# A decoder layer in one kernel: the first group's split and load orders, the weighting of c, q2c as columns, and where its products stand

## The reference, cut to what matters

```python
x = x + attn(layernorm(x))                       # attn: layernorm, q,k,v, softmax over channels, projection, + its input
# xattn(c = layernorm(x), q = ctx):
cq = jnp.einsum('bcd,bqd,d->bcq', c, q, w_cq) + b_cq
s = (c @ w_c + b_c)[:, :, None] + (q @ w_q + b_q)[:, None, :] + cq
a = jax.nn.softmax(s, axis=2)
c2q_att = jnp.einsum('bcq,bqd->bcd', a, q)
b_att = jax.nn.softmax(jnp.max(s, axis=2), axis=1)
q2c_att = jnp.einsum('bc,bcd->bd', b_att, c)[:, None, :]
z = jnp.concatenate([c, c2q_att, c * c2q_att, c * q2c_att], axis=-1) @ W_l.T + b_l
x = x + z
x = x + ffn(layernorm(x))                        # 8 routed experts, 4 of them per token, and a shared one
```

## Time and profile before

| | |
|---|---|
| median of three runs | 799.65 us |
| the profiled execution | 801.21 us |
| its span, first to last instruction | 799.3 us |
| busy: PE / DVE / ACT / POOL | 90% / 65% / 49% / 44% |
| mean granted clock of TensorE | 0.955 |
| attention part, to the first expert product | 487 us |
| period of a loop group | 56.13 us |

### The profile page before, as it was taken

How to read it: one execution, slowest core, us unless ns; L and a number is a source line. 1 busy time by engine, 2 the same in 40 slices (tenths; PEclk the granted TensorE clock), 3 DMA queues, 4 the chain that set the end, 5 groups by cost and what they waited for, 6 DMA issues and landing times. The chain is left out here.

```text
span 799.3 us, 13107 instructions
## 1 busy us (share of the span) xinstructions
PE 716.6 (90%) x4448; PEld 625.8 (78%) x4448; DVE 516.1 (65%) x1309; ACT 392.8 (49%) x856; POOL 355.0 (44%) x450
## 2 busy tenths in 40 slices
PE   3488989989989979989899896699999999999997
PEld 2288878978977868878788795488888888888886
DVE  4577577477576675775774785577667676767533
ACT  3465665755846745746656552343334343434221
POOL 1636565764663764675657620213232323222231
PEclk9888999989999999989999898799999999999999
DMA  8640230330420411402300106602222222221200
GB/s 213 160 122 1 82 121 1 100 100 0 124 76 0 145 55 45 141 13 77 123 0 21 50 1 182 211 1 107 80 106 80 107 79 106 79 106 54 107 27 27
DMA packets 50896, 64.48 MB, mean 81 GB/s; under 512 B 3928, under 2 KB 49544, under 8 KB 49968
## 3 DMA queue, kind: packets, MB, share of 16 engines
q1 hardware_dynamic: 50864, 64.07, 25.3%
HBM read 56.61 MB, written 7.45 MB: 80 GB/s over the span
## 5 line engine op out<-in xcount | busy, mean ns | idle before, releaser
L1356 POOL TENSOR_TENSOR sg<-sg,cw_wide 128x512 f32<-128x512 f32 x56 | 73.5, 1313 | 187.0 <-ACT sg L1313 177.2
L1317 ACT ACTIVATE a_hi<-af 128x512 fp32r<-128x512 f32 x63 | 39.8, 632 | 154.9 <-DVE af L1437 154.9
L772 POOL TENSOR_TENSOR ctxt_lo<-ctxtf,ctxt_hi 128x750 fp32r<-128x750 f32 x32 | 55.2, 1724 | 104.7 <-ACT ctx_hi L595 89.1
L76 PE MATMUL bank<-h_hi,w_lo 128*128 128x512 f32 x224 | 92.5, 413 | 7.3 <-DVE w_lo L1454 5.9
L77 PE MATMUL bank<-h_lo,w_hi 128*128 128x512 f32 x224 | 90.3, 403 | 0.0
L78 PE MATMUL bank<-h_hi,w_hi 128*128 128x512 f32 x224 | 89.9, 401 | 0.0
L1437 DVE TENSOR_TENSOR af<-bank,sg 128x512 f32<-128x512 f32 x63 | 43.2, 686 | 62.2 <-POOL sg L1356 59.1
L1442 DVE TENSOR_TENSOR a_lo<-af,a_hi 128x512 fp32r<-128x512 f32 x63 | 48.1, 763 | 34.9 <-ACT a_hi L1317 34.9
L76 PE MATMUL bank<-w_hi,a_lo 128*128 128x256 f32 x224 | 63.3, 283 | 0.0
L77 PE MATMUL bank<-w_lo,a_hi 128*128 128x256 f32 x224 | 63.3, 283 | 0.0
L78 PE MATMUL bank<-w_hi,a_hi 128*128 128x256 f32 x224 | 63.2, 282 | 0.0
(11 more groups left out here) (260 smaller groups left out, 2336.4 us busy)
## 6 DMA issues: line engine op xcount, KB each, us to landing
cw_wide<-cw_scratch SPq DMA_DIRECT2D x7, 2048.0 KB, 7.1
ctxtf<-in_ctx_t SPq DMA_DIRECT2D x32, 375.0 KB
ctxf<-in_ctx SPq DMA_DIRECT2D x32, 375.0 KB
xt<-in_x SPq DMA_DIRECT2D x8, 448.0 KB, 3.8
x_scratch<-x2b SPq DMA_DIRECT2D x8, 448.0 KB, 7.1
x2n<-x_scratch SPq DMA_DIRECT2D x7, 512.0 KB, 4.7
x2t<-x_scratch SPq DMA_DIRECT2D x7, 512.0 KB, 4.0
out_dram<-x2t SPq DMA_DIRECT2D x7, 512.0 KB, 2.9
```

The lines of the kernel that those rows point to most:

```text
L76: pe.matmul(dst, a_lo, b_hi, start=first, stop=False, **kw)
L772: pool.tensor_tensor(ctxt_lo[:, j, :, 0:S], ctxtf[:, j, :, :], f32(ctxt_hi[:, j, :, 0:S]), ALU.subtract)
L1317: act.activation(a_hi[n % (AHEAD + 1)][:, :], af[(p + n) % 2][:, :], ACT.Copy).then_inc(a_hi_ok, 1)
L1356: pool.tensor_tensor(sg[b][:, :], sg[b][:, :], cw_wide[p][:, ORDER[n], :], ALU.mult).then_inc(sgw_ok, 1)
```

## The change

Group 0: the bias rows are added last in `qk_product`, so that only they wait for the bias; W_p is loaded earlier and split behind the q/k results; W_l is split in four parts through the group; the constants are loaded in an early and a late set; contexts 1 to 3 are split inside the group, not ahead of it. All groups: c is weighted on ScalarE (the high part, straight from ct) and on VectorE (ctw, for the low part), not on GpSimd; q2c is computed as columns, one small product per stream and half, which takes the place of the masked matrix bm, the row copy and the transposes back; `z_q2c` of streams 2 and 3 moves behind `attention_out(2)` and `turn_c(0)`, `z_c(0)` ahead of `turn_c(3)`; `context_hi(i, 3)` moves behind `probs_proj_high(3)` on ScalarE and `context_lo(i, 3)` behind `rstd2(3)` on GpSimd; VectorE takes the statistics of the next x ahead of the similarity maxima, and `x2_sum` of the second pair inside the c stage.

The diff, cut:

```diff
                 load_context(0, 0)
+                sp.dma_start(wp_f[:, :, :], proj_wt.rearrange("(k p) n -> p k n", p=P)).then_inc(wp_in, 16)
                 load_context(0, 1)
...
                     def qk_product(j):
                         pe.wait_ge(h_lo_ok, ev[j])
-                        pe.matmul(bank[j][0:L, :], two_ones[:, :], qk_rows[:, :], start=True, stop=False)
...
+                        if j == 0 and is_first(i):
+                            pe.wait_ge(rows_ok, 1)
+                        pe.matmul(bank[j][0:L, :], two_ones[:, :], qk_rows[:, :], start=False, stop=True).then_inc(qk_mm, 1)
...
+                    z_c2q(0)
+                    pe.wait_ge(b4_ok, i + 1)
                     for j in range(G):
-                        last = pe.matmul(m_bank[0:G, D:2 * D], bm[:, j, :], c[:, j, :], start=(j == 0), stop=(j == G - 1))
+                        for k in range(KB):
+                            last = pe.matmul(m_bank[:, D + k * G + j:D + k * G + j + 1], c[:, j, k * P:(k + 1) * P], b4[:, j:j + 1],
+                                             start=True, stop=True)
                     last.then_inc(q2c_mm, 1)
...
                     exps(3)
-                    if not is_first(i):
-                        context_hi(i, 3)
-                    v_high(0)
...
                     probs_proj_high(3)
+                    if not is_first(i):
+                        context_hi(i, 3)
                     c_high(0)
+                    c_weighted_high(0)
...
+                    if is_first(i):
+                        context_hi(i, 3)
+                        for part in range(1, G):
+                            wl_high(part)
...
                     residual_bias(i)
-                    context_lo(i, 2)
-                    context_lo(i, 3)
+                    if not is_first(i):
+                        context_lo(i, 2)
...
                     rstd2(3)
-                    c_weighted(0)
-                    c_weighted(1)
-                    c_weighted(2)
-                    c_weighted(3)
+                    if is_first(i):
+                        context_t_lo(i, 2)
+                        context_t_lo(i, 3)
+                        context_r_lo(2)
+                        context_r_lo(3)
+                    else:
+                        context_lo(i, 3)
...
                     c_rows(2)
+                    if not is_first(i):
+                        x2_sum(i - 1, 1)
+                    c_low(0)
                     c_rows(3)
...
+                    c_weighted(0)
                     c_low(1)
                     c_weighted_low(0)
...
+                    if is_first(i):
+                        for part in range(1, G):
+                            wl_low(part)
...
+                    if not last:
+                        for j in range(G):
+                            ln1_stats(i + 1, j)
+                        ln1_moments(i + 1)
+                    sim_max(0)
                     row_term(0)
```

More of the change, by code:

```diff
@@ L213, in decoder_layer @@
             b3, b_sum = sb("b3", [L, 3]), sb("b_sum", [L, 1])
[L214 to L215 removed]
+            mhalf, eps, one, mone = (sb(n, [L, G]) for n in ("mhalf", "eps", "one", "mone"))
             xt = sb("xt", [L, G, D])
@@ L423, in v_product @@
                         pe.wait_ge(h_lo_ok, ev[G - 1])
+                        if half == 0 and is_first(i):
+                            pe.wait_ge(bias_ok, 2)
                         n = slice(2 * D + half * P, 2 * D + (half + 1) * P)
@@ L473, in similarity, with turn_a, c2q_product, turn_x @@
                         last.then_inc(s_mm, 1)
+                    def turn_a(j):
+                        pe.wait_ge(exp2_ok, ev[j])
+                        for b in range(NSB):
+                            last = pe.transpose(bank[j][0:SB, b * L:(b + 1) * L], tmp[j][0:L, b * SB:(b + 1) * SB], ident[0:L, 0:L])
+                        last.then_inc(t_a, 1)
+                    def c2q_product(j):
+                        pe.wait_ge(cx_lo_ok, ev[j])
+                        pe.wait_ge(a_lo_ok, ev[j])
+                        for b in range(NSB):
+                            t = slice(b * L, (b + 1) * L)
+                            last = mm3(pe, bank[j][0:L, 0:D], op_hi[j][0:SB, t], op_lo[j][0:SB, t], ctx_hi[:, j, b, :],
+                                       ctx_lo[:, j, b, :], b == 0, b == NSB - 1)
+                        last.then_inc(c2q_mm, 1)
+                    def turn_x(j):
+                        pe.wait_ge(x3_ok, ev[j])
+                        for k in range(2 * KB):
+                            last = pe.transpose(bank[j][:, k * L:(k + 1) * L], tmp[j][0:L, k * P:(k + 1) * P], ident[0:L, 0:L])
+                        last.then_inc(t_x, 1)
+                    def z_c2q(j):
+                        pe.wait_ge(x_lo_ok, ev[j])
+                        for k in range(2 * KB):
+                            t = slice(k * L, (k + 1) * L)
+                            mm3(pe, z_of(j), op_hi[j][:, t], op_lo[j][:, t], wl_hi[:, KB + k, :], wl_lo[:, KB + k, :], False, False,
+                                skip_group_check=True)
                     qk_product(0)
@@ L507, in group @@
                     z_c(2)
+                    turn_a(0)
                     z_c(3)
-                    for j in range(G):
-                        pe.wait_ge(exp2_ok, ev[j])
-                        for b in range(NSB):
-                            last = pe.transpose(bank[j][0:SB, b * L:(b + 1) * L], tmp[j][0:L, b * SB:(b + 1) * SB], ident[0:L, 0:L])
-                        last.then_inc(t_a, 1)
+                    turn_a(1)
+                    turn_a(2)
+                    turn_a(3)
+                    c2q_product(0)
@@ L556, in group @@
-                    z_c2q(0)
                     z_c2q(1)
@@ L634, in v_high @@
                         act.wait_ge(v_mm, KB * i + half + 1)
+                        if half == 0 and is_first(i):
+                            act.wait_ge(bias_ok, 2)
                         act.activation(v_hi[:, half, :], v_bank[half][:, 0:TOK], ACT.Identity,
@@ L648, in c_weighted_high, with wl_high @@
                     def c_weighted_high(j):
-                        act.wait_ge(ctw_ok, ev[j])
-                        act.activation(cw_hi[:, j, :, :], ctw[:, j, :, :], ACT.Copy).then_inc(cw_hi_ok, 1)
+                        act.wait_ge(ct_ok, ev[j])
+                        for k in range(KB):
+                            w = act.activation(cw_hi[:, j, k, :], ct[:, j, k, :], ACT.Identity, bias=wq[:, k:k + 1], scale=wcq[:, k:k + 1])
+                        w.then_inc(cw_hi_ok, 1)
+                    def wl_high(part):
+                        if part == 0:
+                            act.wait_ge(wl_in, 16)
+                        n = slice(part * KB, (part + 1) * KB)
+                        act.activation(wl_hi[:, n, :], wl_f[:, n, :], ACT.Copy).then_inc(wl_hi_ok, 1)
                     if not is_first(i):
```

292 lines of the change are left out of this document (137 added, 155 removed).

## The result

The changed kernel took 814.81 us (median of four runs, 811.12 to 818.34) beside 799.97 for the kernel before: a ratio of 1.0192, interval 1.017 to 1.0213. So it is 1.5 to 1.9% slower; 812 was forecast. The profiled execution took 816.41 us, with a span of 814.6.

A forecast was written before the change was run, and what follows sets the result against it. TensorE, busy 90% of the span, was taken to bound, leaving only idle and slow-clock stretches. First group -12.5, loop +28.9 (six times 4.8) and last group -4.5 gave +11.9 on 799.65: 811.5, say 812 us; range 785 to 828.

The forecast's parts named there:

- wait of x2b: Sign in the loop: GpSimd's x2b sums wait for the store, 4 to 7 us each in six groups.
- wait for h: Sign in the loop: TensorE waits 4 to 6 us for h at the first transposes.
- limit at which it was to fall: Forecast falls if x2b does not wait or the period is under 57; first-group term, if scores start after 30.
- rival 2: Loop: the wait is there, but clock and ports cost nothing; period 57.5, total 791 us; chance 13%.
- rival 3: First group gains half, because of the W_l split and its contention with GpSimd; 820 to 828 us; chance 10%.
- The chain of the store: Loop: last root, context 3's low part, late store, x2b sums, scalars, then h; period 60.95 against 56.13 us.
- The sharing: Loop: context 3's low part on GpSimd slowed beside VectorE's SBUF work, +1.2 us, bounds 0 and 2.
- The c stage: Loop: similarity ends 3.6 us sooner, context product over at 244, not 247.6; gain ends in the wait for h.
- the first rival: Loop: the store does not bind; period 51.4, total 754 us, 772 with the port lock; chance 15% for both.
- Half clock: Loop: TensorE's hole before the transposes of h lowers the clock behind it; 2.25 us a group, bounds 0 and 3.4.
- The first group: Group 0: earlier q/k products and scores, less the W_p and W_l splits; 12.5 us gained, between 8 and 16.
- The last group: Last group: no new wait, context product starts 4.4 us earlier; 4.5 us gained, between 1 and 6.

The follow-up runs named there:

- context 3 early: The changed kernel with context 3 split where it was before the change, on ScalarE and GpSimd: 791.77 us, ratio 0.9903 to the kernel before.
- Freed of both faults: Context 3 split early, store first, waits in group 0 for bias rows and W_l, and ScalarE's context 3 split behind stream 1's probability product: 778.51 us, ratio 0.9741.
- the repeat: The changed kernel itself, unaltered, run once more beside the kernel before: 811.17 us, ratio 1.0152.
- the experiment: The changed kernel, but in group 0 GpSimd makes the row parts of contexts 2 and 3 behind VectorE's last W_l parts: 807.32 us, ratio 1.0092.
- all repairs: The changed kernel with context 3 split early, the store ahead of the last context load, and two GpSimd waits in group 0: 788.29 us, ratio 0.9864.

## Why the prediction was right, point by point

Sign and size were right, 812 forecast and 811 to 815 measured, and so was the move in the loop that loses the time. The way was half right: the late x2b store binds as forecast, but the held c(3) binds about as much, and moving the store alone gave back 1.2 to 2.5 us a group of the 2.6 to 3.9 that undoing the whole move gave. The total is closer than its parts by luck: -12.5, +28.9, -4.5 were forecast for first group, loop and last group, -4.2, +18.3, +0.8 came, errors of +8.3, -10.6 and +5.3 us that leave 3.0.

Of the signs that the forecast named, the wait of x2b was longer (8.5 to 9.05 us in place of 4 to 7), the wait for h shorter (1.3 to 1.8 in place of 4 to 6), the period 59.19 and 57.86 in place of 60 to 62, and the scores came at 28.05, not at 25 to 27. No limit at which it was to fall was reached. Two of its rivals were in part true at once: the loop came near rival 2 (a period of 57.5 without sharing and clock), and the first group gained less than the half that rival 3 gave it. Rival 2 alone gave 791 us and rival 3 alone 820 to 828; together they left the forecast's number.

**The chain of the store** (26.1 + 3.5 + 1.3 + 7.15 + 2.8 + 4.55) came as priced: 26.13, 3.42, 1.43, 7.16, 2.97, 4.34. From the normalise to the first z_c2q product it took 4.61, not 4.1. So group 2, at 58.53 us, is 2.4 under the forecast's 60.95 by the sharing (1.2) and by what follows the first z_c2q product (8.47 in place of 8.0 + 2.25), less that 0.5.

**The sharing, +1.2 on this chain,** was put on the wrong engine. GpSimd's split took 3.42 us, no longer than before; VectorE paid. Here the forecast had weighed the Trainium skill (SBUF — State Buffer, "Who interferes with whom"), which calls the shared port pair an exclusive lock held for the whole instruction, and dismissed it with the words that in the sum neither matters since the chain has 5.3 us of slack. The traces of the loop agree with the Trainium skill: the held instructions end 0.07 to 0.25 us behind GpSimd's, and the one that reads a bank is not held. The forecast also put the cost on c's low parts, of which c_lo, with its operand in a bank, is not held at all (0.38), and not on c(3), which is (3.13). It mattered because the slack was not there.

**The c stage** is the step that failed. The walk had the product with the context over at 244, 41.15 us into the group; it was over at 44.9, as before (44.8). c(0) did come 1.45 us sooner, but c(3) ended 1.3 later for GpSimd's sake, and, with c(3) ending when it did before, the interleaved products and the weighting on other engines won 0.6 us at the similarity (30.0 with context 3 early, 30.6 at best before) and 0.15 at the start of the product with the context (40.28, 40.43). The walk had 3.6 for each. So TensorE waited 1.3 to 1.8 us for h, not 4 to 6. Freed of both faults the period is 53.77, not the 51.4 of the first rival.

**Half clock, 2.25 behind the hole at h:** the hole was 1.3 to 1.8 us, and from the first z_c2q product it is 8.47 us to the next group where 8.0 was forecast without it; 9.48 from the product at 137.32 in group 1. In the repeat it was 7.9 to 8.2, with nothing lost. So the term measured 0 to 1.5 us, not 2.25, and a low clock stood also at a place where the forecast had put none, behind the hole of c(3) (0.75 over 13.5 us, 0.87 to 1.00 with c(3) short).

**The first group.** The scores came at 28.05, not 25.4. The 3.4 us of the bias rows did not come: VectorE made them beside GpSimd's split of context 0, 4.0 us for what takes 1.1, and ScalarE waits for w_q until 24.76 anyway, which the forecast overlooked. In the repeat the scores came at 27.17. W_l was the larger miss: priced at 2 us net with "up to twice" the 0.7 per part, the parts took 1.9 us each, and of the 10.3 us by which the first z_c product behind the similarity was ahead (60.82 against 71.14) 4.2 were left at the product with the context (70.72 against 74.87): 6.2 us, of which the experiment gave 1.2 to 2.6 back. The cause of the rest was not tested.

**The last group:** forecast -4.5 from an earlier context product, measured +0.8: c(3) is held there too. Without that it is 59.1 with all repairs, 0.6 less than before, so most of the 4.5 was, it seems, the same overestimate of the c stage.

## What to carry to other kernels

Before an instruction of GpSimd is moved, lay it over VectorE's queue at the new place: a sum, a scaling or a cast that works on SBUF alone there can last until GpSimd is done, and a wait of 3 us can fall on the one instruction that TensorE needs. Ask in which queue the semaphore it posts is waited for, and what stands behind that wait: here a load, then a store, then a buffer, then the next group. When a chain is declared to have slack, so that a cost beside it "doesn't matter", price that chain with the same care as the binding one.

## What the runs showed of the hardware

A normalise of 112 x 256 on VectorE took 0.41 us alone and 3.13 beside two instructions of GpSimd in a row: it was not let in between them (first ends 233.30, second 235.06, the held one 235.21). Such a one can also be let in: in the first group of the changed kernel the first of the two row steps shown started beside context 0's first instruction (ends 18.76) and was over at 19.31, while the second instruction took 2.25 us in place of 1.85. Even a cast of one partition with 512 elements took 1.91 us in place of 0.42. An instruction with one operand in PSUM took 0.38 us beside the same neighbours, and statistics of a tile in SBUF 0.41 to 0.43, 0.40 alone. The store of 448 KB landed 7.1 us after its issue right behind two context loads, and after 3.3 without them. GpSimd itself lost little: 3.42 us for the split of context 3 beside c(3) as alone, though 2.1 us in place of 1.85 for each row part beside W_l. Two kernels with the same instructions in the same order and one idle wait of difference gave 814.8, 811.2 and 809.9 us in three sets of runs; in their profiles single groups of the loop take 57.5 to 60.4 us.
